# A decoder layer on one core: new hand-written orders for the attention bodies, and an own order for the last body but one

## What is computed

```python
x = _layernorm(x + _L0_attn_ref(x, Wq, Wk, Wv, fc_w, fc_b))          # 3 heads of width 512, mean over heads
x = _layernorm(x + _L0_xattn_ref(x, ctx, Wq, Wkv_expand, Wout))      # 16 heads of width 32, causal
x = _layernorm(x + _L0_ffn_ref(x, ...))                              # 64 experts, top 6, capacity 128, plus a shared FFN
```

## Time and profile before

| | us |
|---|---|
| median of three runs | 2055.18 |
| lowest, highest | 2049.06, 2066.52 |
| the run that was profiled | 2054.85 |
| its span, first to last instruction | 2053.1 |

### The profile page before, as it was taken

How to read it: one execution, slowest core, us unless ns; L and a number is a source line. 1 busy time by engine, 2 the same in 40 slices (tenths; PEclk the granted TensorE clock), 3 DMA queues, 4 the chain that set the end, 5 groups by cost and what they waited for, 6 DMA issues and landing times.

```text
span 2053.1 us, 42835 instructions
## 1 busy us (share of the span) xinstructions
...
## 2 busy tenths in 40 slices
...
DMA packets 202021, 285.59 MB, mean 139 GB/s; under 512 B 100283, under 2 KB 110523, under 8 KB 201820
## 3 DMA queue, kind: packets, MB, share of 16 engines
...
HBM read 208.67 MB, written 57.42 MB: 130 GB/s over the span
## 4 chain that ended last, share of the span: by engine, by line
PE 67%; DVE 24%; DMA 3%; issue 3%; ACT 2%; SPq 1%; POOL 0%; DVEq 0%; ACTq 0%; POOLq 0%
PE moe_bank L1731 26%; PE ring L932 26%; DVE quad L1314 5%; PE moe_bank L1800 4%; DVE inv_denominator L1330 3%; DMA x1T_split<-x_rows_split 3%; PE fold L485 3%; PE quad L1039 2%; DVE scratch L1335 2%; DVE scratch L1266 2%; PE moe_bank L1766 1%; DVE maxima L1314 1%; PE moe_bank L1778 1%; DVE pre_norm L1289 1%; PE ring L1056 1%
## 5 line engine op out<-in xcount | busy, mean ns | idle before, releaser
L178 POOL DMA_INDIRECT slot_table<-table_records,slot_of_choice x204 | 233.0, 1142 | 259.6 <-DVE slot_of_choice L1402 171.7
L902 POOL TENSOR_SCALAR_AFFINE_SELECT scratch<-scratch 128x1024 f32<-128x1024 f32 x64 | 74.5, 1163 | 561.2 <-ACT scratch L1188 561.2
L932 PE MATMUL ring<-xT_split,tion_then_expert_weights 128*128 128x256 f16 x2304 | 267.0, 273 | 0.0
L932 PE MATMUL ring<-tion_then_expert_weights,xT_split 128*128 128x512 f16 x1152 | 264.6, 379 | 0.0
L932 PEld LDWEIGHTS ring<-xT_split,tion_then_expert_weights 128*128 128x128 f16 x2304 | 221.9, 98 | 33.1 <-DVE score_rows L1276 2.4
L1680 POOL DMA_INDIRECT expert_sums<-tion_then_expert_weights,scatter_index x64 | 135.7, 2120 | 199.0 <-DMA expert_sums<-tion_then_expert_weights,scatter_index 70.6
L1168 ACT ACTIVATE scratch<-ring 128x512 f16<-128x512 f32 x192 | 112.6, 595 | 186.1 <-PE ring L932 184.4
L932 PEld LDWEIGHTS ring<-tion_then_expert_weights,xT_split 128*128 128x128 f16 x1152 | 110.3, 98 | 122.7 <-issue 2.9
L1314 DVE CUSTOM_DVE_ANT_0 quad<-quad,causal_penalty 128x128 f32<-128x128 f32 (+1 forms) x512 | 165.7, 396 | 14.2 <-PE quad L1022 13.0
L1266 DVE SCALAR_TENSOR_TENSOR scratch<-ring,scratch 128x512 f16<-128x512 f32 x192 | 130.1, 685 | 25.4 <-ACT scratch L1168 23.5
L932 PE MATMUL ring<-scratch,xT_split 128*128 128x256 f16 x1152 | 136.4, 273 | 0.0
...
## 6 DMA issues: line engine op xcount, KB each, us to landing
...
```

What stands on the lines that cost most here:

```text
L178: pool.indirect_dma_start(self.dram, bass.IndirectOffsetOnAxis(ap=self.slot[:, tb, c:c + 1], axis=0), self.record[:, tb, c, :], None, boun ...
L932: last = pe.matmul(out_, left(a, c), right(b, c), start=(n == 0 and not onto), stop=(n == 3 * chunks - 1))
```

## The change

New lists for bodies 1 to 14, for body 16 and for body 17; and lists of its own for body 15 (`PE_PREV`, `ACT_PREV`, `DVE_PREV`, `POOL_PREV`). No step is added or removed, and none changes its shape. The core of the diff (of each table a line or two):

```diff
 PE_BODY = [
-    ("K", 0, 0), ("Y", 0, 0), ("V", 0, 0), ("Y", 0, 1), ("K", 1, 0), ("Q", 0, 0), ("Q", 1, 0), ("S", 0, 0),
+    ("Y", 0, 0), ("Y", 0, 1), ("K", 0, 0), ("C", 0, 0), ("V", 0, 0), ("K", 1, 0), ("Q", 0, 0), ("Q", 1, 0),
...
 DVE_BODY = [
-    ("RM", 0, 0), ("OM", 3, 0), ("CT", 0, 0), ("O", 1, 0), ("LN", 1, 0), ("OUT", 0, 0), ("OUT", 1, 0),
-    ("RS", 0, 0),
+    ("OM", 3, 0), ("RM", 0, 0), ("O", 1, 0), ("LN", 1, 0), ("OUT", 0, 0), ("OUT", 1, 0), ("RS", 0, 0),
...
 SCATTER_BEHIND = [
-    (-1, ("AV", 3, 0)), (-1, ("AV", 3, 0)), (-1, ("O", 1, 0)), (-1, ("OUT", 0, 0)), (-1, ("OUT", 1, 0)), (0, ("V", 0, 0)),
-    (0, ("K", 1, 0)), (0, ("Q", 0, 0)), (0, ("Q", 1, 0)), (0, ("Y", 0, 1)), (0, ("C", 1, 0)), (0, ("Y", 1, 1)),
+    (0, ("K", 0, 0)), (0, ("K", 0, 0)), (0, ("V", 0, 0)), (0, ("V", 0, 0)), (0, ("V", 0, 0)), (0, ("V", 0, 0)),
+    (0, ("V", 1, 0)), (0, ("V", 1, 0)), (0, ("V", 1, 0)), (0, ("V", 1, 0)), (0, ("MT", 0, 0)), (0, ("MT", 0, 0)),
 ]
+SCATTER_BEHIND_LAST = [(-1, ("OUT", 1, 0))] * (NB * TOPK)
...
+PE_PREV = [
+    ("K", 0, 0), ("C", 0, 0), ("K", 1, 0), ("V", 0, 0), ("Q", 0, 0), ("Q", 1, 0), ("M", 0, 0), ("M", 1, 0),
+    ("M", 2, 0), ("M", 3, 0), ("V", 0, 1), ("R", 0, 0), ("MT", 0, 0), ("MT", 1, 0), ("ST", 0, 0), ("ST", 1, 0),
+    ("V", 1, 0), ("ST", 2, 0), ("C", 1, 0), ("ST", 3, 0), ("V", 1, 1), ("AV", 0, 0), ("AV", 1, 0), ("V", 2, 0),
+    ("Y", 0, 0), ("Y", 0, 1), ("S", 0, 0), ("S", 0, 1), ("Y", 1, 0), ("Y", 1, 1), ("AV", 2, 0), ("S", 1, 0),
...
+ACT_PREV = [
+    ("NX2", 0, 0), ("K", 0, 0), ("NX1", 0, 0), ("XH", 0, 0), ("C", 0, 0), ("XH", 1, 0), ("V", 0, 0),
+    ("Q", 0, 0), ("Q", 1, 0), ("K", 1, 0), ("V", 0, 1), ("ZH", 0, 0), ("ST", 0, 0), ("ST", 1, 0), ("RM", 0, 0),
...
+DVE_PREV = [
+    ("ST2", 0, 0), ("LN", 2, 0), ("V", 0, 0), ("XL", 0, 0), ("C", 0, 0), ("XL", 1, 0), ("K", 0, 0), ("Q", 0, 0),
+    ("K", 1, 0), ("Q", 1, 0), ("M", 0, 0), ("M", 1, 0), ("M", 2, 0), ("M", 3, 0), ("ZL", 0, 0), ("R", 0, 0),
+    ("MT", 0, 0), ("V", 0, 1), ("RC", 0, 0), ("MT", 1, 0), ("P", 0, 0), ("C", 1, 0), ("AV", 0, 0), ("V", 1, 0),
...
+POOL_PREV = [
+    ("CS", 0, 0), ("SC", 0, 1), ("XS", 0, 0), ("SC", 1, 1), ("SC", 2, 1), ("MASK", 0, 0), ("MASK", 1, 0),
...
 PE_LAST = [
+    ("CT", 0, 0), ("SG", 2, 0), ("OUT", 0, 0), ("OUT", 1, 0), ("SU", 0, 0), ("SU", 1, 0), ("SG", 3, 0),
+    ("SU", 2, 0), ("SU", 3, 0), ("SG", 4, 0),
...
 PE_TAIL = [
-    ("SU", 2, 0), ("SU", 3, 0), ("SG", 4, 0), ("R", 0, 0), ("SU", 4, 0), ("CT", 0, 0),
+    ("R", 0, 0), ("SU", 4, 0), ("CT", 0, 0),
...
-X_READERS = [s for s in PE_BODY if s[0] in ("Y", "V", "S")]
-CTX_READERS = [s for s in PE_BODY if s[0] in ("K", "C")]
-CTX_READERS_LAST = [s for s in PE_LAST if s[0] in ("K", "C")]
+X_SPLIT_BEHIND, CTX_SPLIT_BEHIND = ("O", 0, 0), ("OUT", 0, 0)
...
+                                              (PE_PREV, ACT_PREV, DVE_PREV, POOL_PREV) if self.is_(B - 1) else
...
-                    pool.wait_ge(full, b.last_job(*X_READERS[-1]))
+                    pool.wait_ge(full, b.last_job(*X_SPLIT_BEHIND))
...
-                        pool.wait_ge(full, b.last_job(*CTX_READERS[-1]))
+                        pool.wait_ge(full, b.last_job(*CTX_SPLIT_BEHIND))
```

More of the change, by code:

```diff
@@ L538 @@
 SCATTER_BEHIND = [
[L539 to L546 removed]
[3 rows of a table removed]
+    (0, ("K", 0, 0)), (0, ("K", 0, 0)), (0, ("V", 0, 0)), (0, ("V", 0, 0)), (0, ("V", 0, 0)), (0, ("V", 0, 0)),
+    (0, ("V", 1, 0)), (0, ("V", 1, 0)), (0, ("V", 1, 0)), (0, ("V", 1, 0)), (0, ("MT", 0, 0)), (0, ("MT", 0, 0)),
+]
+SCATTER_BEHIND_LAST = [(-1, ("OUT", 1, 0))] * (NB * TOPK)
+POOL_BODY = [
+    ("XS", 0, 0), ("CS", 0, 0), ("SC", 0, 1), ("SC", 1, 1), ("SC", 2, 1), ("SC", 3, 1), ("SC", 4, 1),
+    ("SC", 5, 1), ("SC", 6, 1), ("SC", 7, 1), ("SC", 8, 1), ("SC", 9, 1), ("SC", 10, 1), ("SC", 11, 1),
+    ("MASK", 0, 0), ("MASK", 1, 0), ("MASK", 2, 0), ("MASK", 3, 0),
+]
+PE_PREV = [
[6 rows of a table added]
+]
+ACT_PREV = [
[6 rows of a table added]
+]
+DVE_PREV = [
[8 rows of a table added]
+]
+POOL_PREV = [
[3 rows of a table added]
 ]
 PE_LAST = [
[4 rows of a table removed]
[5 rows of a table added]
 ]
 ACT_LAST = [
[6 rows of a table removed]
[5 rows of a table added]
 ]
 DVE_LAST = [
[6 rows of a table removed]
[L572 to L574 removed]
[6 rows of a table added]
+]
+POOL_LAST = [
+    ("SC", 0, 1), ("CS", 0, 0), ("SC", 1, 1), ("SC", 2, 1), ("SC", 3, 1), ("SC", 4, 1), ("SC", 5, 1),
+    ("SC", 6, 1), ("SC", 7, 1), ("SC", 8, 1), ("SC", 9, 1), ("SC", 10, 1), ("SC", 11, 1), ("MASK", 0, 0),
+    ("MASK", 1, 0), ("MASK", 2, 0), ("MASK", 3, 0),
 ]
 PE_TAIL = [
[L577 removed]
+    ("R", 0, 0), ("SU", 4, 0), ("CT", 0, 0),
 ]
 ACT_TAIL = [
[L580 to L581 removed]
+    ("NX2", 0, 0), ("ZH", 0, 0), ("SH", 0, 0), ("GC", 3, 0), ("SH", 1, 0), ("SG", 2, 0), ("SH", 2, 0),
+    ("SG", 3, 0), ("RM", 0, 0), ("SG", 4, 0), ("SH", 3, 0), ("SH", 4, 0),
 ]
 DVE_TAIL = [
[L584 to L586 removed]
[3 rows of a table added]
 ]
@@ L728, in __init__ @@
                                               (PE_FIRST, ACT_FIRST, DVE_FIRST, POOL_BODY) if self.is_(0) else
+                                              (PE_PREV, ACT_PREV, DVE_PREV, POOL_PREV) if self.is_(B - 1) else
                                               (PE_BODY, ACT_BODY, DVE_BODY, POOL_BODY)))
-            self.ring = [s for s in self.pe if s[0] in RING_STEPS or self.is_(B) and s[0] == "SG"]
+            self.ring = [s for s in self.pe if s[0] in RING_STEPS or s[0] == "SG" and s[1] < EARLY_RING]
+            self.pool_splits = [s[0] for s in self.pool if s[0] in ("XS", "CS")]
             self.split = [s for s in self.act if s[0] in SPLIT_STEPS]
```

25 lines of the change are left out of this document (8 added, 17 removed), and 85 rows, old and new, of tables (ACT_BODY, ACT_LAST, ACT_PREV, DVE_BODY).

## The result

The changed kernel takes 2093.01 us (median of four runs, 2085.37 to 2100.21) against 2055.67 for the kernel before: 1.016 times as long, interval 1.011 to 1.021. The forecast was 2098. The run that was profiled took 2093.03 us, its span 2091.3, against 2054.85 and 2053.1. So the direction and the size came as forecast. The stages didn't all: two terms of the sum were off by 22 and 10 us, in opposite directions, and that the total came within 6 us is in part luck.

The account below looks back on a forecast made before the run. TensorE was taken to bound the repeated body (70.95 of 73.1 us busy). From 2054.85 us, -10 for bodies 1 to 14, +53 for body 15 and +1 for bodies 16 and 17 gave 2098 us, range 2062 to 2114.

Parts of the forecast that it names:

- The idle terms: Body 15: TensorE's waits, listed step by step, sum to 52.8 us idle, against about 4 before.
- ahead of Q: Body 15: Q comes 21.0 us after OUT 1 of body 14 instead of 9.5, with TensorE idle for 16.4.
- the last group: Body 15: waits of ST 1, ST 3, AV 1 and two S steps, together 11.6 us.
- the rival: CS and XS hold LN 1 and LN 2: +9 us over 14 bodies, up to 3 in body 15; 2110 us, chance 0.15.
- The lower clock: Body 15: steps after idle gaps run slower; 1.7 for Q, 2.6 for V 1, 1.7 for what follows, +6 us.
- a body -0.7: Bodies 1 to 14: waits removed less waits added give -0.7 us each, ends 0 and -1.9; -10 us in all.
- the sign I had set for being wrong: Wrong if repeated bodies are under 71.3 us, or Q of body 15 comes within 12 us of OUT.
- the floor: Rival: repeated bodies gain all of 1.9 us 14 times (-27), body 15 costs +45; 2068 us, chance 0.17.
- the collision with OM: Repeated bodies: XS holds OM for 2.15 us instead of 0.4; removing this removes OUT's 1.4 us wait.
- Bodies 16 and 17: Last bodies: 83 us plus about 4 for the lower clock, against 86.1; +1 us, ends -5 and +6.
- Faster: Rival: VectorE's work sets the last bodies, which end 16 us sooner if it stays as busy; 2029 us, chance 0.06.
- does little: Rival: body 15's waits overlap, Q, M and R half as long, +18 us in all; 2063 us, chance 0.07.

Follow-up runs that it names:

- experiment 1: Changed kernel without body 15's own order, so body 15 runs by the common lists: 2035.67 us, 0.987 of the kernel before.
- experiment 5: Changed kernel with GpSimd running XS ahead of CS and SC 0 in body 15: 2142.53 us, run once on another chip; Q at 19.8 us instead of 22.7.
- Experiment 3: As experiment 1, but with the repeated lists and scatter places of before, keeping the new starts of XS and CS: 2067.25 us, 1.005 of the kernel before.
- 4: As experiment 1, with the new repeated lists but the old starts of XS and CS: 2045.17 us, 0.994 of the kernel before.
- 11: Changed kernel, body 15 by the common lists, last-body and tail lists of before except GpSimd's last list: 2025.38 us, 0.986 of the kernel before.
- 12: As 11, with CS ahead of SC 0 on GpSimd in body 16: 2026.59 us, 0.983 of the kernel before.

## Why the prediction was right, and where it was not

The terms were off by -22, +10, +4 and +2 (the experts), which add up to -6: the total is better than its parts.

**Body 15 decides, by its own order: right, and shown** (1). The idle terms: 52.8 forecast, 53.6 measured. One by one, forecast to measured: ahead of Q 16.4 to 16.2; M 0 2.6 to 2.5; the three M 9.0 to 8.7; R 8.2 to 7.5; ST 0 5.0 to 4.9; the last group 11.6 to 13.7 (ST 3 3.5 to 5.4).

**The first of them is right by two errors that cancel.** Q was forecast at +21.0 and came at +22.7. LN 2 was late by 3.0 us of hold, which I had put into the rival and not into the sum; XL to Q took 5.3, not 5.9. TensorE was busy 1.9 longer (V at 1.2 GHz), so that the idle share came out the same. The prediction set the rule on two SBUF inputs against the change, and L203, which multiplies rstd by itself, bears it out: beside CS it takes 0.51 instead of 0.16 (end of body 14 in the profile after).

```profile
1114.39 0.34 DVE L194 TENSOR_SCALAR root_tmp<-root_tmp 128x2 uint32<-128x2 uint32 x1
...
1114.97 0.51 DVE L203 TENSOR_TENSOR root_tmp<-rstd 128x2 f32<-128x2 f32 x1
```

The steps that cost the 3.0 us have only one input, so that rule doesn't name them. The Trainium skill (SBUF — State Buffer, Who interferes with whom) has `tensor_scalar` among the kinds that can take the ports that VectorE shares with GpSimd, when its operands meet further conditions. The traces agree as to the kind: L193 and L195 of body 15 and L194 above wait to the end of the GpSimd instruction beside them. By experiment 5 the price is 2.9 us in body 15, the rival's "up to 3". In a repeated body it is 0.5 us in LN 1, and Q doesn't wait for it: the rival's 9 us didn't come. Experiment 3 shows how near that rival was: with the old lists Q does wait 0.6 longer. The profile before already had a hold of this kind, by SC: L194 of LN 2 takes 0.32 us from 790.47 instead of 0.17 and ends with the SC of 789.83, and so in eleven other bodies (0.32 to 0.42).

**The lower clock: mis-sized.** Forecast +6. The body by the common lists has 70.6 us of work (71.2 less 0.6 idle, experiment 1); 139.5 - 70.6 - 53.6 = 15.3 us go neither to work at full clock nor to waits of over 0.5. Against the same steps at 2.4 GHz in other profiles, the slow rows add up to 14.7 of them. I had counted Q, V 0 1 and 1.7 of the rest; in fact nearly every step behind a wait pays, V 0 0 1.7, Q 1.9, V 0 1 2.0, V 1 0 2.3, V 2 0 2.1, V 1 1 0.8, R 0.5, and the M, ST and AV steps 3.3 together. Only the first rows of M 0 and the S steps don't. The granted clock was at 1.2 GHz for about 61 of the 139.5 us. Not all of the 15.3 is lost time: V 0 0's 1.7 lie inside Q's wait, and filling the waits gave 5.9 of 137.8 back. How the rest divides between the 1.2 GHz left in that run (0.95 on average), the cost of the fillers and waits that take over wasn't separated. With what the body before lost itself (6.2: 76.8 - 70.6) this makes 53.6 + 15.3 - 6.2 = 62.7, the measured difference.

**The repeated bodies: wrong.** The step "a body -0.7" failed; it was -2.0 from Q to Q, and the sign I had set for being wrong, under 71.3, was met. Removed as forecast: OUT's 1.37 and ST 0's 0.32. Forecast as added: 0.4 for AV 0 and Q, which didn't come; AV 0 waits in two bodies only (0.3 and 0.4), and Q's own 0.22 went away. M 0, M 2 and M 3 added 0.36 net instead of 0.6. That makes 1.6 less waiting. The remaining 0.43 is busy time (70.95 to 70.52 with the same matmuls), which the trace doesn't explain. Besides, four of the bodies before took 74.1 to 74.8, which I hadn't counted, where after shows 71.5 at most: 1.0 to 1.7 above their like, so that the mean over bodies 1 to 14 is -2.3. I had seen that five new waits might each be small and gave the floor 0.17; what held it back was adding an upper end for each. Experiments 3 and 4 show that the reason given, the collision with OM, is half of it (1.1 of 2.0, and only with starts and lists together); the lists bring the other 0.9 by themselves.

**Bodies 16 and 17: +5.3, forecast +1.** R's 7.43 fell to 3.56, not to nothing, since the six steps behind OUT were through before the x2 DMAs landed. And K waits 6.85 for CS behind SC 0, a GpSimd queue that I hadn't walked. Moving CS gives 4.7 us with the old last lists (11, 12); with the new ones it wasn't tried.

**Faster, does little:** neither; XL of body 15 came at +17.4 (1134.12), where +4 was the point from which the first decides, and Q, M and R waited in full.

**Readings that don't hold.** The 28.8 us idle from 1159 us on aren't more than in all other bodies together: from Q of body 1 to the end of body 14 TensorE was idle for 33.9 us (1018.46 less 984.56 busy). Rows 4 and 5 show no GpSimd instruction beside OUT's readings or a reciprocal; elsewhere in that profile a reciprocal (770.12, 1.76 us, its usual time) does stand beside XS's first half. 2098.9 is 2099. None of these moves the forecast.
